# Leaf column on GpSimd, first scores in slots with the first tree groups, a tree group every three slots, attention of the routed network at two slots a tile

## The reference

```python
out = x + attention(xn) + ffn(xn)
# attention: 16 heads of width 8; scores + relative position bias; softmax; @ v; projection
# ffn:
xn2 = (xn - mean) / sqrt(std + 1e-5)
q, k, v = fff_q(xn2), fff_k(xn2), fff_v(xn2)      # three routed trees, relu
y = xn2 + softmax(q @ k.T / sqrt(128)) @ v        # one head of width 128, per batch
ffn = y + fff_f(y)                                # a fourth routed tree, gelu
# fff: eight levels of a binary tree choose one of 256 leaves for each token;
#      act(x @ w1[leaf] + b1[leaf]) @ w2[leaf] + b2[leaf], w1 is 128 x 16
```

## Time and profile before

| | us |
|---|---|
| median of three runs | 713.75 (712.23 to 715.29) |
| profiled execution | 716.28 |
| its span, first to last instruction | 714.6 |
| TensorE busy | 576.0 (81%) |
| VectorE busy | 441.7 (62%) |
| ScalarE busy | 336.8 (47%) |
| GpSimd busy | 255.1 (36%) |

### The profile page before, as it was taken

How to read it: one execution, slowest core, us unless ns; L and a number is a source line. 1 busy time by engine, 2 the same in 40 slices (tenths; PEclk the granted TensorE clock), 3 DMA queues, 4 the chain that set the end, 5 groups by cost and what they waited for, 6 DMA issues and landing times.

```text
span 714.6 us, 11516 instructions
## 1 busy us (share of the span) xinstructions
PE 576.0 (81%) x3540; PEld 413.1 (58%) x3540; DVE 441.7 (62%) x1024; ACT 336.8 (47%) x738; POOL 255.1 (36%) x242
## 2 busy tenths in 40 slices
PE   2276644799999999999999898998976898989930
PEld 0164532577777777776767655656643466666620
DVE  2959987657576666666667556555768565555300
ACT  5520001455555545464646554545223378878720
POOL 4401766750006578267003820000000776000285
PEclk9998758899999999999999999999999799999985
DMA  7979541275657778788551210000000357445123
GB/s 222 253 170 218 215 134 44 54 198 154 163 148 207 195 196 164 184 186 188 155 160 42 34 16 15 1 1 1 0 1 0 112 111 168 133 134 143 41 34 76
DMA packets 108828, 83.42 MB, mean 117 GB/s; under 512 B 8688, under 2 KB 105840, under 8 KB 108768
## 3 DMA queue, kind: packets, MB, share of 16 engines
q1 hardware_dynamic: 93472, 70.07, 37.0%
q0 software_dynamic: 15104, 12.63, 9.6%
q10 hardware_dynamic: 192, 0.00, 0.0%
HBM read 58.30 MB, written 24.36 MB: 116 GB/s over the span
## 4 chain that ended last, share of the span: by engine, by line
PE 59%; DVE 8%; issue 5%; ACT 5%; POOL 4%; DMA 0%; POOLq 0%; DVEq 0%; ACTq 0%
PE ps L983 8%; PE ps L960 7%; PE ps L971 7%; PE ps L973 7%; PE ps L1037 7%; PE ps L1047 6%; POOL xr L386 3%; PE ps L943 3%; DVE ps L618 2%; PE ps L1090 2%; PE ps L1042 2%; ACT hr L797 2%; PE ps L1031 2%; PE ps L998 1%; PE ps L1097 1%
## 5 line engine op out<-in xcount | busy, mean ns | idle before, releaser
L618 DVE CUSTOM_DVE_ANT_0 ps<-ps,strip 128x512 f32<-128x512 f32 x256 | 176.9, 701 | 132.7 <-PE ps L960 128.4
L786 ACT ACTIVATE pt<-ps 128x512 f32<-128x512 f32 x256 | 150.7, 600 | 91.1 <-PE ps L973 89.4
L381 POOL DMA_INDIRECT xs<-xr,slot x64 | 63.4, 990 | 244.6 <-issue 154.8
L971 PE MATMUL ps<-qs,km 128*128 128x512 f32 x256 | 127.1, 497 | 8.4 <-ACT pt L786 7.5
L960 PE MATMUL ps<-km,qs 128*128 128x512 f32 x256 | 111.8, 443 | 15.9 <-DVE mx L618 7.4
L386 POOL DMA_INDIRECT yt<-ys,slot x48 | 74.6, 1555 | 80.5 <-DMA ys<-yl 66.5
L797 ACT ACTIVATE hr<-ps,wt 128x128 f32<-128x128 f32 x192 | 54.7, 368 | 68.0 <-PE ps L1037 68.0
L973 PE MATMUL ps<-u_lo,rev_r 128*128 128x220 f32 (+1 forms) x256 | 74.5, 291 | 0.0
L973 PE MATMUL ps<-u_hi,rev_r 128*128 128x220 f32 (+1 forms) x256 | 73.2, 286 | 0.0
L983 PE MATMUL ps<-pt,v_aug 128*32 128x512 f32 x512 | 69.0, 612 | 0.7 <-ACT pt L786 0.7
L971 PEld LDWEIGHTS ps<-qs,km 128*128 128x128 f32 x256 | 49.0, 191 | 31.2 <-ACT pt L786 19.6
(11 more groups left out here) (207 smaller groups left out, 864.2 us busy)
## 6 DMA issues: line engine op xcount, KB each, us to landing
wt<-in_wl SPq DMA_DIRECT2D x192, 128.5 KB, 2.4
xl<-xs SPq DMA_DIRECT2D x48, 258.0 KB
ys<-yl SPq DMA_DIRECT2D x48, 256.0 KB
xs<-mx SPq DMA_DIRECT2D x2, 3096.0 KB, 23.7
strip<-bias_bf SPq DMA_DIRECT2D x1, 3584.0 KB, 36.2
u_hi<-bias_hi SPq DMA_DIRECT2D x1, 2496.0 KB, 16.1
u_lo<-bias_lo SPq DMA_DIRECT2D x1, 2496.0 KB, 28.5
xs<-xr,slot POOLq DMA_INDIRECT x64
```

The source lines that it names most:

```text
L381: pool.indirect_dma_start(out=xs[t % 2][:, :], out_offset=bass.IndirectOffsetOnAxis(ap=slot[:, t, k:k + 1], axis=0), in_=xr[:, k, :], in_o ...
L618: V.tensor_tensor_reduce(out=bank(u % banks), in0=bank(u % banks), in1=strip[:, HG * g + j, b0:b0 + NS], scale=1.0, scalar=LOWEST, op0=ALU ...
L786: A.activation(pt[:, kt % 2, j, :], bank(2 + u % 2), ACT.Exp).then_inc(S["ex"], 1)
L971: T.matmul(bank(2 + u % 2), km[:, par, j, kt * P:(kt + 1) * P], qs[:, par, :], start=True, stop=False)
```

## The change

The numbers of the order change: three slots a group instead of four, x at 0, h at 1, m at 2, y at 4; the 36 groups begin 16 slots ahead of slot 0, among the first scores of step 0, which become slots -20 to -1 over two banks; transposes of q and k at one slot each from 95, attention at two slots a tile from 103, routing of tree f from 138, its groups from 190. The leaf's place in its block is kept for each tree (`part_of`), and GpSimd copies it into `xr` ahead of each scatter; VectorE's wait for the scatter goes. The gather of v signals four tokens' columns at a time (`g_v0` to `g_v3`), and o waits for those of its own batch.

```diff
-STAGE_AT = {"x": 0, "h": 2, "m": 3, "y": 5}
-EVERY = 4
-QK_FROM, ATT_FROM, ROUTE_FROM, F_FROM = 150, 167, 209, 252
-ATT_PE, ATT_DVE, ATT_ACT = {"s": 0, "p": 2, "o": 4}, {"s": 0, "o": 4}, {"s": 1, "p": 2}
+STAGE_AT = {"x": 0, "h": 1, "m": 2, "y": 4}
+EVERY = 3
+TREES_FROM, QK_FROM, ATT_FROM, ROUTE_FROM, F_FROM = -16, 95, 103, 138, 190
+ATT_PE, ATT_DVE, ATT_ACT = {"s": 0, "p": 2, "o": 3}, {"s": 0, "o": 3}, {"s": 1, "p": 2}
...
-        for first, start, count in ((0, 0, NTREE * GROUPS), (NTREE * GROUPS, F_FROM, GROUPS)):
+        for first, start, count in ((0, TREES_FROM, NTREE * GROUPS), (NTREE * GROUPS, F_FROM, GROUPS)):
...
-    t, rest = divmod(slot_ - QK_FROM, 2)
-    return [t] if rest == 0 and 0 <= t < 2 * NB else []
+    t = slot_ - QK_FROM
+    return [t] if 0 <= t < 2 * NB else []
...
-    return [... if ATT_FROM + 5 * i // 2 + d == slot_]
+    return [... if ATT_FROM + 2 * i + d == slot_]
...
+                settle(G.tensor_copy(xr[:, :, P], part_of[:, t, :]))
                 for k in range(NT):
...
-                    fetch(yt[:, t, k, :], ys[t], slot[:, t, k:k + 1], ALU.add, S["g_y"])
-                pool.wait_ge(S["g_y"], 16 * NT * (t + 1))
+                    fetch(yt[:, t, k, :], ys[t], slot[:, t, k:k + 1], ALU.add, S["g_y"] if t < 2 else S[f"g_v{k // KT}"])
+                if t < 2:
+                    pool.wait_ge(S["g_y"], 16 * NT * (t + 1))
...
-                V.tensor_copy(slot[:, t, :], st[:, 5, :])
-                if t:
-                    dve.wait_ge(S["d_sc"], 16 * NT * t)
-                V.tensor_copy(xr[:, :, P], whole[:, 0:NT]).then_inc(S["sl"], 1)
+                V.tensor_copy(slot[:, t, :], st[:, 5, :]).then_inc(S["sl"], 1)
...
-            for u in range(U):
-                scores_q(0, u, 0, 4)
+            for at in range(SLOTS):
+                if at >= LAG:
+                    scores_q(0, at - LAG, 0)
+                for k, i in stages(slot_of(-1, at)):
+                    stage(k, i, i % 2)
...
-                    if i == 0:
-                        pe.wait_ge(S["g_y"], 16 * NT * 3)
+                    if c == 0:
+                        pe.wait_ge(S[f"g_v{b_}"], 16 * KT)
```

More of the change, by code:

```diff
@@ L92, in qk_at @@
 def qk_at(slot_):
-    t, rest = divmod(slot_ - QK_FROM, 2)
-    return [t] if rest == 0 and 0 <= t < 2 * NB else []
+    t = slot_ - QK_FROM
+    return [t] if 0 <= t < 2 * NB else []
 def attend(delays, slot_):
-    return [(k, i) for i in range(NT) for k, d in reversed(delays.items()) if ATT_FROM + 5 * i // 2 + d == slot_]
+    return [(k, i) for i in range(NT) for k, d in reversed(delays.items()) if ATT_FROM + 2 * i + d == slot_]
 def window(kt):
@@ L172, in build @@
         st = sb("st", [P, 8, NT])
-        whole = sb("whole", [P, NT + BLK], I32)
+        whole = sb("whole", [P, BLK], I32)
+        part_of = sb("part_of", [P, NTREE + 1, NT], I32)
         ewc = sb("ewc", [P, NTREE + 1], I32)
@@ L207, in build @@
             "lx0 lx1 lw0 lw1 st xT xTs hh hr mk hm yy yl d_nf yT_ps yT_sb "
-            "g_y g_b g_o0 g_o1 g_o2 g_o3 t_ps t_sb s_ps s_mx s_ex pT_ps pT_sb o_ps y_sb y_add dv d_out").split()}
+            "g_y g_v0 g_v1 g_v2 g_v3 g_b g_o0 g_o1 g_o2 g_o3 t_ps t_sb s_ps s_mx s_ex pT_ps pT_sb o_ps y_sb y_add dv d_out").split()}
         LX, LW_ = (S["lx0"], S["lx1"]), (S["lw0"], S["lw1"])
@@ L559, in route @@
                 then(V.tensor_scalar(leaf[:, t, :], st[:, 4, :], float(LEAVES * t), None, ALU.add))
-                then(V.tensor_scalar(whole[:, 0:NT], leaf[:, t, :], LB - 1, None, ALU.bitwise_and))
+                then(V.tensor_scalar(part_of[:, t, :], leaf[:, t, :], LB - 1, None, ALU.bitwise_and))
                 yield
@@ L564, in route @@
                 c = lambda i, n=BLK: sm[:, i, 0:n]
-                then(V.tensor_scalar(whole[:, NT:NT + BLK], ps[:, rank[1], 0:BLK], float(P - 1), None, ALU.add))
-                then(V.tensor_scalar(whole[:, NT:NT + BLK], whole[:, NT:NT + BLK], -P, None, ALU.bitwise_and))
-                then(V.tensor_copy(c(0), whole[:, NT:NT + BLK]))
+                then(V.tensor_scalar(whole[:], ps[:, rank[1], 0:BLK], float(P - 1), None, ALU.add))
+                then(V.tensor_scalar(whole[:], whole[:], -P, None, ALU.bitwise_and))
+                then(V.tensor_copy(c(0), whole[:]))
                 yield
@@ L610, in split_k, with row_max @@
                     V.tensor_scalar(km[:, par, j], ks[:], hmask[:, j:j + 1], None, ALU.mult).then_inc(S["km"], 1)
-            def row_max(n, g, u, banks=2):
+            def row_max(n, g, u):
                 qt, j = divmod(u, HG)
@@ L617, in row_max @@
                 b0 = P * qt
-                V.tensor_tensor_reduce(out=bank(u % banks), in0=bank(u % banks), in1=strip[:, HG * g + j, b0:b0 + NS],
+                V.tensor_tensor_reduce(out=bank(u % 2), in0=bank(u % 2), in1=strip[:, HG * g + j, b0:b0 + NS],
                                        scale=1.0, scalar=LOWEST, op0=ALU.add, op1=ALU.max,
@@ L715, in _ @@
             dve.wait_ge(S["d_z"], 32)
-            for u in range(U):
-                row_max(0, 0, u, 4)
+            for at in range(SLOTS):
+                if at >= LAG:
+                    row_max(0, 0, at - LAG)
+                for k, i in stages(slot_of(-1, at)):
+                    stage(k, i)
             sub_max(0, 0)
@@ L947, in project, with scores_q @@
                 last.then_inc(S["proj"], 1)
-            def scores_q(n, u, par, banks=2):
+            def scores_q(n, u, par):
                 qt, j = divmod(u, HG)
@@ L955, in scores_q @@
                     pe.wait_ge(S["km"], HG * n + j + 1 + CREDIT["km"])
[L956 to L960, removed]
+                pe.wait_ge(S["max"], U * n + u - 1 + CREDIT["max"])
+                T.matmul(bank(u % 2), qs[:, par, qt * P:(qt + 1) * P], backward(km[:, par, j, :]), start=True, stop=True
                          ).then_inc(S["p1"], 1)
```

## The result

The changed kernel takes 744.1 us (742.48 to 747.72), the kernel before, on the same chip, 713.7; the ratio is 1.0432, with a 95% interval of 1.0388 to 1.0477. The forecast was 744. The profiled execution took 743.74 us, with a span of 742.0. In the kernel after, h is L1040, m L1045, y L1050, x L1034, the weight loads L265, the first scores L963, the second L974, p L1100.

What follows compares the result with a forecast made beforehand. TensorE's work bounds the loop, GpSimd's last gather the end. Terms -4 + 33 + 20 - 6 + 3 + 3 - 19 = +30 on the 714.6 us span, corrected to 744 us; range 718 to 765, eight in ten 708 to 778.

Steps and rivals of the forecast that it cites:

- The four pieces of the table: Span cut at first score, maxima and TensorE's end; differences forecast at -4, +20, +33 and -19 us.
- Leaf column: Routing before the first scores: VectorE no longer waits for the scatter before copying the column, -4 us.
- First scores as slots: First score to maxima: five groups run among the first scores, waiting for weights; +20 us, bounds +12 to +30.
- Tree groups in the loop: Loop: 26 periods each wait 1.7 us for weights, +44, less 11.3 for groups moved out; +33 us.
- Attention: Routed network's attention at two slots a tile: p waits less for VectorE's add; -6 us, bounds -11 to +2.
- Last tree: Last tree's groups: weight waits of 15.3 us replace 12.4 us too much before; +3 us, bounds -5 to +10.
- Bare slots: Slots without tree work: 3.75 more bare steps at 0.8 us each; +3 us, bounds 0 to +5.
- The tail: End of the kernel: last gather done well before TensorE ends, then only VectorE's add and what follows; -19 us, firm.
- (1): Rival: the weight loads land in time and the wait vanishes; -41 us, 673 us, chance 0.12.
- (2): Rival: weight landing always the shortest, 2.2 us, borders covering more; -15 to 0, 700 to 714 us, chance 0.14.
- (3): Rival: h and y fall into the slow stretch, half of 35 periods 1.6 us longer; +28, 770 us, chance 0.14.
- (4): Rival: values' gather, or scatter and rows of tree 2, late; one wait of 5 to 15 us, inside the forecast's range.

Runs made afterwards that it cites:

- `three_buffers`: Changed kernel with a third weight buffer, group n+3's weights loaded after y(n): 715.5 us, ratio 1.003 to the kernel before.
- `store_first`: Changed kernel, two weight buffers, with SyncE issuing a group's store ahead of the next weight loads: 822.5 us, ratio 1.147 to the kernel before.
- `three_store_first`: Changed kernel with a third weight buffer and a group's store issued ahead of the weight loads: 711.5 us, ratio 0.997 to the kernel before.
- `four_plain`: Changed kernel at four slots a group with the old distances, tree groups begun at slot 0 instead of -16: 703.8 us, ratio 0.987 to the kernel before.
- `two_loads`: Changed kernel with only two of a group's four weight loads issued after the first groups: 711.6 us, ratio 0.996 to the kernel before.
- `four_slots`: Changed kernel with four slots a group and the old distances within a group: 687.1 us, ratio 0.963 to the kernel before.

## Why the prediction was right, and where its working was not

The forecast of 744 us against 744.1 is closer than its working. The four pieces of the table missed by -2.7, +2.6, +0.9 and -3.4 us and cancelled to -2.6 on the span, and the last step from the span to the median run made up for that; that the number agrees to a tenth is luck. What the trace bears out is the mechanism, that the tail is gained and more than that is lost where the groups stand closer.

- **Leaf column**, forecast -4: -4.4 alone, -6.7 to the first score in the change. Right. The other 2.3 us stay open: in their profiled executions the kernels with groups among the first scores start the first score anywhere from 112.7 to 115.5 us (`three_buffers`, `store_first`), those without at 115.1 to 115.3.
- **First scores as slots**, forecast +20: +22.6. h(2), h(3) and h(4) start 13.1, 21.5 and 28.5 us after the first x (113.32), where 12.0, 18.6 and 25.3 were forecast, each behind the weights (7.7 us of waiting in three places). The 2 us put down for the lower clock were partly due: the granted clock was 0.89 in this piece. Half the loads shorten the piece to 27.3 us, so some 6.8 of its 34.1 are the weights' turn-round; with a third buffer it is 32.2, and 29.2 with the store first.
- **Tree groups in the loop**, forecast +33. Taken over the steps with tree groups, and with 22.45 us a step for their bare slots: before, 268.5 us in eight steps leave 88.9; after, 231.7 in five leave 119.5; that is +30.6. The sum is right, and its reason is half right. The turn-round was priced well (5.2 us against 5.0), but the wait is this less the work in between, and that step failed: "3 x 0.87 + 0.71 = 3.3 us of TensorE work".

  In the trace without a wait for weights (`three_store_first`) the time from y(n) to h(n+2) is 4.55 us at the median, 3.65 where no weighing falls between. A weighing falls between in 17 of the 28 cases of groups 5 to 32; the prediction had a figure for it, "4.2 where the slots are full and hold a weighing", and took 3.3 for all.

  Two things were missing. The price of a slot was an average over the step, the cheap half slots at its border among it; away from the border it is 0.84 and a quarter of a weighing, 1.09, so 4.0 us for three slots, m and x, and, as an estimate, a wait of 1.0 us, 27 us for the 26 periods, near the weights' 25; the trace has 24.0 us in 18 places.

  The rest is the waits that the forecast put at nothing, "Everything shorter in the cycle (...) falls inside this wait". Where the weights wait only 0.65 us longer than the rest (5.20 less 4.55), it doesn't: m behind yl and h behind xTs cost about 0.3 us hidden and 0.3 us shown in a group. 25 us for the weights and some 18 to 22 for the rest, the hand-overs in the main, stand where 44 were put down for the weights alone; the two errors cancelled in the sum, and that is luck.
- **Attention**, forecast -6: -4.3 alone, at p's wait as expected; p waits 3.0 us in four places in the changed kernel.
- **Last tree**, forecast +3: its steps take 34.61, 45.27 and 31.27 us, 15.6 more than bare slots and twelve groups by the forecast's price; 12.4 before, so +3.2.
- **Bare slots**: 22.43 and 22.45 us a step, 22.3 forecast. What is left of the piece from the maxima to TensorE's end, when the three terms above are taken out, is 33.9 - 30.6 + 4.3 - 3.2 = 4.4 us, where +3 was forecast.
- **The tail**, forecast -19: -22.4. Right in its chain (TensorE, VectorE's add, the output); what follows the last add was copied from before, and is shorter now.
- **Rivals.** (1), loads in time, was priced wrongly at 673 us: without a wait for weights the kernel takes 711 us, since the hand-overs at one slot are left. The 25 us of the weights' wait in 5 to 35 do vanish in that run, as the rival said; its price forgot what stands behind. (2) fell: from y(n) to h(n+2) the median was 5.2 us, and not the 4.2 of the shortest landing. (3): in 5 to 35 the clock falls three times, to 0.98 in the mean, for some 5 us of TensorE's busy time by the comparison above, where the rival had 28; `store_first` shows it further down, at 0.90. (4): TensorE's list holds no wait for the values' gather of the changed kernel's attention; a late gather came in another place, at the end of `four_plain`.
- **Sensitivity.** "1 us there is 35 to 40 us of time" is no single slope. Half the loads, with their issues done 1.0 us sooner (0.90 instead of 1.93 us), gained 32 us in `two_loads`; 1.15 us more ahead of the loads cost 78 us in `store_first`, some 68 us for a microsecond, because 39 groups wait instead of 25 and a period grows by more than the delay.

## What to carry to other kernels

Before groups are packed closer, compare for every buffer the time from its release to its next use, in slots at their local price, with issue and landing of its refill: three slots were 0.65 us short here for the weights (4.55 us of room by the medians, 5.20 needed), four had room (8.6 us), and the same change at four slots is 4% faster than the kernel before instead of 4% slower. A hand-over between engines that gets one slot instead of two costs a few tenths of a microsecond that the list of waits doesn't show; it is read from the start of one matmul to the start of the next, beside the same pair without a hand-over. When a wait is taken away, price the next one in the same cycle before counting the gain.

## What the runs showed of the hardware that was not expected

- TensorE's granted clock follows its waits in a loop that is busy most of the time: in the stretch 5 to 35 it is 1.00 in `four_slots` (busy 199.91 of 204.60 us), 0.98 in the changed kernel (182.30 of 215.10) and 0.90 in `store_first` (198.36 of 267.40), where it falls to the lower level, 1.2 GHz, twelve times and returns to 2.4.
- Half the weight loads of a group (`two_loads`) do not remove the wait, but leave 5.6 us in 8 places; a third buffer (`three_buffers`), which takes the load out of the chain from y(n) to h(n+2), does.
